# Attention in a macaron block: probabilities times V as three split passes for the 256-column blocks, with a new order of a head pair

## The chip, the cores and the metric

The kernel runs on one core of one Trainium2 chip. The metric is the device time of one execution in microseconds (us), lower is better; the time of a kernel is the median of its runs. TensorE (PE) multiplies 128x128 stationary weights with a moving operand and writes to the accumulation memory (PSUM, eight banks of 128x512 fp32). VectorE (DVE) and ScalarE (ACT) read and empty PSUM, GpSimd (POOL) works on the on-chip memory only, SyncE (SP) issues transfers. Each engine runs its own program in order, and they meet at semaphores.

## The reference, cut to what matters

```
x = x + 0.5 * ffn(layernorm(x))          # mixture of 8 experts (top 2) and a shared one
x = x + attention(layernorm(x))          # x: 4 batches x 256 tokens x 256
x = x + 0.5 * ffn(layernorm(x))

def attention(x):                        # 16 heads of 128
    q, k, v = x @ W_Q + b_Q, x @ W_K + b_K, x @ W_V + b_V
    scores = q @ k.T / sqrt(128)         # causal mask within 256 tokens
    z = softmax(scores) @ v
    return z @ W_O + b_O
```

All of it is in fp32. Where the kernel works with "split operands", a value is held as a high part that the faster fp32r format represents and a low part, the difference; a product is then three passes, high x high, high x low and low x high.

## The kernel before

The first feed-forward stage, the attention and the second feed-forward stage follow each other, each in its own block of instructions with a meeting of all engines between them. The change is in `attention()` alone.

The attention runs over 8 pairs of heads (pair 0 written out, the others in loops on each engine; on some engines the last pair is written out too). Within a pair the work is named by letter and number, and four strings give each engine the order of its own items: `ORDER` (PE), `ACT_ORDER`, `DVE_ORDER`, `POOL_ORDER` (lines 1224 to 1233). The numbers stand for these items:

- A0 to A3, B0 to B3: projections to Q and K of the two heads, for the first (A) and second (B) 512 tokens, 6 passes of 512 columns each. ACT or DVE adds the bias and writes `qk`.
- V0 to V3: projection to V for batch 0 to 3, both heads, 12 passes of 256 columns. ACT (V0, V2) or DVE (V1, V3) copies all 512 columns to `v`.
- S, K, E, R, P, T, M, Z, L, each with a unit number 0 to 7 (unit u is batch u // 2, head u % 2). S: scores on PE, fp32, a 128x128 block for the first 128 queries and a 128x256 block for the others. K: mask and row minimum on DVE (`masked`). E: exponential with row sum on ACT (`exps`). R: reciprocal on DVE (`recip`). P: product with it on POOL (`probs`). T: three 128x128 transposes on PE (`turn`), then a copy of the 384 columns to `pT` on ACT (`turned`). M: probabilities times V on PE (`mix`), fp32: keys 0 to 127 against all 256 queries, then keys 128 to 255 against the last 128. Z and L: high and low part of the result, on ACT (`z_high`) and DVE (`z_low`).
- O0 to O3: output projection of a batch, 12 passes of 256 columns, added to `x_res` on DVE (`added`). O3 of a pair is done in the next pair; in pair 0 its place on DVE holds the second half of the layer norm's application, and PE skips it.
- w0 to w5: POOL splits a sixth of the next pair's projection weights (`split_qkv`, two instructions of 256 columns). W0: the same for the output projection's weights (`split_out`), and in pair 0 also the addition of the output bias to `x_res` (`out_bias`, line 1291).

A, B, V and O write to banks 0 and 1 in turn (`BANKED`, `BANK`): item number n of that list waits until the item n - 2 has been emptied (`bank_free`, line 1477). In pair 0, where O3 is skipped, the item two places after it looks one further round back. Scores use banks 3 and 4, transposes 5 and 6, M banks 2 and 7. S0 waits for A0 to A3 to be written, S4 for B0 to B3 (`projected`). A pair begins on PE with a wait for the weights w0 to w3 (`s_ql`), V0 with one for w4 and w5. In pair 0 PE turns the second half of the normalised input before V0, ACT makes its high part (`norm_high`) and DVE its low part ahead of K0 (`norm_low`); B0 waits for both:

```python
if fresh and item == "K0":
    norm_low(dve, n, 1, (5, 6))
```

In the last pair DVE also takes the statistics of the next layer norm (ahead of L6, after O1 has been added) and applies it (ahead of O2); POOL computes the root in between.

## Time and profile before

| | us |
|---|---|
| median of 3 runs | 542.2 |
| the runs | 541.19, 542.2, 546.09 |
| the profiled execution | 542.72 |
| its span, first to last instruction | 540.8 |
| busy: PE / DVE / ACT / POOL | 515.3 / 326.7 / 268.6 / 273.6 |

The profile is one execution. Its times are in us from the span's start unless marked ns. A group of instructions is named by the line of the kernel, which may be that of a helper: L179 to L181 are the three passes of `split_matmuls`, L1560 and L1561 the two products of `mix`, L1542 the transposes, L1532 and L1533 the scores. An fp32 matmul leaves two records. The arrow gives the releaser of an idle time. A matmul is drawn until its modelled end, which lies past the start of the next.

### The profile page before, as it was taken

How to read it: one execution, taken by the hardware profiler on the slowest of the kernel's cores; microseconds unless marked ns; L12 is line 12 of the kernel's file. 1: busy time of each engine (PE TensorE's matmuls, PEld its weight loads, DVE VectorE, ACT ScalarE, POOL GpSimd, SP SyncE). 2: the span in 40 equal slices, each digit the busy share in tenths (PEclk: the TensorE clock that was granted, in tenths of full speed). 3: DMA queues.
4: the chain of work that ended last, by engine and by line, in shares of the span. 5: the costliest groups of instructions: out<-in, count | busy, mean ns of one | idle time of the engine just before them, and what ended most of it. 6: DMA issues, size and time to landing. Idle time of an engine off the chain costs nothing. (4 is left out here: it accounts for less than half of the span.)

```text
span 540.8 us, 10506 instructions
## 1 busy us (share of the span) xinstructions
PE 515.3 (95%) x3318; PEld 460.3 (85%) x3319; DVE 326.7 (60%) x821; ACT 268.6 (50%) x731; POOL 273.6 (51%) x364
## 2 busy tenths in 40 slices
PE   7999699997989999999999999999999799899996
PEld 4788599976879999898999998999999688799985
DVE  5689655548646564574655645746656768755537
ACT  3982356540554463563544635535456365355540
POOL 1737777751295372570843725718333221667750
PEclk9999799998999999999999999999999999999999
DMA  8941223342101001001010010010000140223327
GB/s 280 348 143 31 68 93 104 107 157 63 55 19 59 1 19 61 19 0 58 19 58 2 18 58 19 0 58 19 0 1 0 49 137 1 69 87 101 106 88 234
DMA packets 19401, 37.99 MB, mean 70 GB/s; under 512 B 2864, under 2 KB 10416, under 8 KB 19376
## 3 DMA queue, kind: packets, MB, share of 16 engines
q1 hardware_dynamic: 14960, 25.61, 14.4%
q0 software_dynamic: 4416, 12.06, 6.9%
q8 instruction: 14, 0.23, 0.2%
q14 instruction: 11, 0.09, 0.1%
HBM read 28.49 MB, written 9.18 MB: 70 GB/s over the span
## 5 line engine op out<-in xcount | busy, mean ns | idle before, releaser
L1315 POOL TENSOR_TENSOR s_a<-s_a,rr_a 128x128 f32<-128x128 f32 x64 | 25.5, 399 | 137.1 <-DVE rr_a L1422 137.1
L1362 ACT ACTIVATE s_a<-s_a,mn_a 128x128 f32<-128x128 f32 (+1 forms) x128 | 56.7, 446 | 14.9 <-DVE mn_a L1416 14.9
L179 PE MATMUL bank<-xT_h,area_h 128*128 128x512 f32 x128 | 53.7, 420 | 3.4 <-PEq L1171 3.4
L1412 DVE SCALAR_TENSOR_TENSOR s_a<-bank,cst 128x384 f32<-128x384 f32 x64 | 35.3, 551 | 35.3 <-PE bank L1533 35.1
L521 POOL DMA_INDIRECT xn<-x_normed,tok_i_f x46 | 45.7, 993 | 16.8 <-issue 10.2
L180 PE MATMUL bank<-xT_l,area_h 128*128 128x512 f32 x128 | 50.8, 397 | 0.0
L181 PE MATMUL bank<-xT_h,area_l 128*128 128x512 f32 x128 | 50.6, 396 | 0.0
L1355 ACT ACTIVATE qk_a<-bank,bias_a 128x512 f32<-128x512 f32 x32 | 21.9, 683 | 55.6 <-PE bank L181 55.6
L1367 ACT ACTIVATE pT_a<-bank 128x384 f32<-128x384 f32 x64 | 31.1, 486 | 34.5 <-PE bank L1542 33.6
L1404 DVE TENSOR_SCALAR qk_a<-bank,bias_a 128x512 f32<-128x512 f32 x32 | 24.0, 751 | 37.5 <-PE bank L181 37.5
L179 PE MATMUL bank<-area_h,xT_h 128*128 128x256 f32 x128 | 40.7, 318 | 0.0
L1428 DVE SCALAR_TENSOR_TENSOR area_l<-bank,bias_a,area_h 128x256 fp32r<-128x256 f32 x64 | 30.4, 477 | 17.0 <-ACT area_h L1372 17.0
L1416 DVE TENSOR_REDUCE mn_a<-s_a 128x1 f32<-128x128 f32 (+1 forms) x128 | 39.2, 347 | 2.2
L179 PE MATMUL bank<-w_h,xeT_h_f 128*128 x92 | 34.5, 375 | 5.6 <-DVE xeT_l_f L802 5.6
L1317 POOL TENSOR_TENSOR s_a<-s_a,rr_a 128x256 f32<-128x256 f32 x64 | 39.2, 612 | 0.0
L1560 PE MATMUL bank<-pT_a,v_a 128*128 128x256 f32 x128 | 39.1, 387 | 0.0
L179 PE MATMUL bank<-area_h 128*128 128x256 f32 x128 | 38.2, 298 | 0.6 <-issue 0.6
L527 POOL DMA_INDIRECT y_by_token<-rows_f,place_f x32 | 31.5, 985 | 13.4 <-issue 7.9
L1533 PE MATMUL bank<-qk_a 128*128 128x256 f32 x128 | 38.2, 381 | 0.0
L1372 ACT ACTIVATE area_h<-bank,bias_a 128x256 fp32r<-128x256 f32 x64 | 29.9, 467 | 14.2 <-PE bank L1561 14.2
L179 PE MATMUL bank<-xT_h,wgu_h 128*128 128x512 f32 x88 | 35.8, 407 | 1.0 <-DVE hT_l_f L706 1.0
L181 PE MATMUL bank<-area_h,area_l 128*128 128x256 f32 x128 | 36.3, 283 | 0.0
(176 smaller groups left out, 1652.3 us busy)
## 6 DMA issues: line engine op xcount, KB each, us to landing
area<-in_wqkv SPq DMA_DIRECT2D x8, 768.0 KB, 4.4
xn<-y_by_token SPq DMA_DIRECT2D x12, 256.0 KB, 3.7
w_r<-in_w SPq DMA_DIRECT2D x8, 352.0 KB
area_r<-in_w SPq DMA_DIRECT2D x16, 176.0 KB
x_normed<-xn SPq DMA_DIRECT2D x4, 512.0 KB, 5.8
area<-in_wo SPq DMA_DIRECT2D x8, 256.0 KB, 2.6
x_res<-in_x_in SPq DMA_DIRECT2D x4, 256.0 KB, 4.1
wgu_r<-in_wgu SPq DMA_DIRECT2D x4, 256.0 KB
```

Of the source, the lines that this page charges most:

```text
L179: pe.matmul(psum, lhs[0], rhs[0], start=first, stop=False)
L180: pe.matmul(psum, lhs[0], rhs[1], start=False, stop=False)
L181: return pe.matmul(psum, lhs[1], rhs[0], start=False, stop=last)
L521: pool.indirect_dma_start(xe[m % XR], None, xd, bass.IndirectOffsetOnAxis(ap=tok_i[:, m:m + 1], axis=0)).then_inc(s_xe[m % XR], 16)
L527: pool.indirect_dma_start(yd, bass.IndirectOffsetOnAxis(ap=place[:, m:m + 1], axis=0), ye[m % YR], None).then_inc(s_yst[m % YR], 16)
L1317: pool.tensor_tensor(s[b][:, P:3 * P], s[b][:, P:3 * P], rr[:, b, 1:2].to_broadcast([P, 2 * P]), ALU.mult).then_inc(s_p, 1)
L1362: act.activation(s[b][:, cols], s[b][:, cols], ACT.Exp, bias=mn[:, b, t:t + 1], scale=-1.0, accum_out=rs[:, b, t:t + 1]).then_inc(s_e, 1)
L1367: act.activation(pT[u % 2][:, :], bank[5 + u % 2][:, 0:3 * P], ACT.Copy).then_inc(s_ptv, 1)
L1412: dve.scalar_tensor_tensor(s[b][:, :], bank[3 + u % 2][:, 0:3 * P], -INV_SCALE, cst[:, C_MASK:C_MASK + 3 * P], ALU.mult, ALU.max).then_inc ...
L1416: dve.tensor_reduce(mn[:, b, t:t + 1], s[b][:, cols], op=ALU.min, axis=AX.X).then_inc(s_mn, 1)
L1533: pe.matmul(b[:, P:3 * P], q[:, t0 + P:t0 + 2 * P], k[:, t0:t0 + 2 * P], start=True, stop=True).then_inc(s_sc, 1)
L1560: pe.matmul(bank[ZB[u % 2]][:, 0:2 * P], v[:, 2 * bt, e], pT[u % 2][:, 0:2 * P], start=True, stop=False)
```

## The change

Three things are changed together. (1) The product with keys 0 to 127 (256 columns) is done in three fp32r passes from split operands; the product with keys 128 to 255 (128 columns) stays fp32. So V's even blocks are held as `v_h` and `v_l`, the odd ones as `v_odd`, and a transposed unit as `pT_h`, `pT_l` and `pT_odd`. (2) ACT copies the odd and the high part, two instructions for each V and each unit; DVE subtracts for the low part, after ACT, in V's items and in a new item Q (`turned_low`), with a new semaphore `s_ptl` that `turn` and `mix` wait on. V is now in ACT's and in DVE's list, and the counts `NA` and `ND` replace `PROJ // 2`. (3) The four orders are new; O3 stands second on PE and first on DVE; O1 on DVE stands behind Q6 and Q7; in the last pair the statistics are ahead of O2 and the application ahead of L7.

```diff
--- before.py
+++ after.py
@@ -1184,7 +1184,9 @@
                 qk = sb("qk", [P, 2, 2, TOK])
-                v = sb("v", [P, NT, 2 * DH])
+                v_h = sb("v_h", [P, BATCH, 2 * DH], FP32R)
+                v_l = sb("v_l", [P, BATCH, 2 * DH], FP32R)
+                v_odd = sb("v_odd", [P, BATCH, 2 * DH])
                 bias = sb("bias", [P, 3, 2])
@@ -1192,7 +1194,9 @@
                 rr = sb("rr", [P, NS, 2])
-                pT = [sb(f"pT{b}", [P, 3 * P]) for b in range(2)]
+                pT_h = [sb(f"pT_h{b}", [P, 2 * P], FP32R) for b in range(2)]
+                pT_l = [sb(f"pT_l{b}", [P, 2 * P], FP32R) for b in range(2)]
+                pT_odd = [sb(f"pT_odd{b}", [P, P]) for b in range(2)]
@@ -1210,6 +1214,7 @@
                 s_ptv = sem("a_pT")
+                s_ptl = sem("a_pT_low")
                 s_z = sem("a_z_psum")
@@ -1221,20 +1226,22 @@
-                ORDER = ("A0 A1 A3 A2 O3 V0 S0 S1 B0 S2 V1 T0 S3 V2 B3 T1 M0 B1 B2 T2 M1 S4 T3 M2 S5 S6 "
-                         "V3 M3 S7 T4 O0 T5 M4 M5 T6 O1 M6 T7 O2 M7").split()
-                ACT_ORDER = ("A0 A2 V0 E0 B0 E1 T0 V2 E2 E3 T1 Z0 B2 T2 Z1 T3 E4 Z2 E5 Z3 E6 T4 T5 E7 Z4 T6 "
-                             "Z5 T7 Z6 Z7").split()
-                DVE_ORDER = ("A1 A3 O3 K0 K1 R0 R1 V1 K2 K3 B3 R2 B1 L0 R3 K4 L1 K5 R4 K6 R5 K7 L2 R6 L3 V3 "
-                             "O0 R7 L4 L5 O1 L6 O2 L7").split()
-                POOL_ORDER = "w4 w5 P0 P1 W0 P2 w0 P3 w1 w2 w3 P4 P5 P6 P7".split()
+                ORDER = ("A0 O3 A1 A2 A3 V0 S0 S1 B0 S2 V1 B2 T0 S3 V2 T1 B1 B3 M0 T2 S4 S5 M1 T3 S6 V3 S7 M2 T4 "
+                         "M3 T5 O0 M4 M5 O1 T6 T7 O2 M6 M7").split()
+                ACT_ORDER = ("A0 A2 V0 B0 E0 E1 V1 T0 B2 E2 V2 T1 E3 Z0 T2 E4 T3 E5 Z1 V3 T4 Z2 Z3 T5 E6 E7 Z4 Z5 "
+                             "T6 T7 Z6 Z7").split()
+                DVE_ORDER = ("O3 A1 A3 V0 K0 K1 R0 K2 V1 R1 Q0 K3 V2 R2 Q1 B1 R3 B3 L0 K4 K5 R4 Q2 Q3 K6 R5 L1 K7 "
+                             "Q4 L2 Q5 L3 R6 V3 O0 R7 L4 L5 Q6 Q7 O1 O2 L6 L7").split()
+                POOL_ORDER = ("w4 w5 P0 P1 P2 P3 w0 W0 P4 P5 w1 P6 P7 w2 w3").split()
                 BANKED = [item for item in ORDER if item[0] in "ABVO"]
...
                 ON_DVE = [item for item in DVE_ORDER if item[0] in "ABV"]
+                NA, ND = len(ON_ACT), len(ON_DVE)
                 PROJECTED = [item for item in ORDER if item[0] in "ABV"]
@@ -1338,8 +1345,6 @@
                     kind, x = item[0], int(item[1])
-                    if kind == "V":
-                        return v[:, 2 * x:2 * x + 2, :].rearrange("p a b -> p (a b)")
                     half = "AB".index(kind)
@@ -1350,7 +1355,8 @@
                         if item[0] == "V":
-                            act.activation(proj_out(item), src, ACT.Copy).then_inc(s_pa, 1)
+                            act.activation(v_odd[:, x, :], src[:, 2 * DH:4 * DH], ACT.Copy)
+                            act.activation(v_h[:, x, :], src[:, 0:2 * DH], ACT.Copy).then_inc(s_pa, 1)
                         else:
@@ -1364,7 +1370,8 @@
                         act.wait_ge(s_pt, U * i + u + 1)
-                        act.activation(pT[u % 2][:, :], bank[5 + u % 2][:, 0:3 * P], ACT.Copy).then_inc(s_ptv, 1)
+                        act.activation(pT_odd[u % 2][:, :], bank[5 + u % 2][:, 2 * P:3 * P], ACT.Copy)
+                        act.activation(pT_h[u % 2][:, :], bank[5 + u % 2][:, 0:2 * P], ACT.Copy).then_inc(s_ptv, 1)
@@ -1399,7 +1406,9 @@
                         if item[0] == "V":
-                            dve.tensor_copy(proj_out(item), src).then_inc(s_pv, 1)
+                            dve.wait_ge(s_pa, NA * i + ON_ACT.index(item) + 1)
+                            dve.tensor_tensor(v_l[:, x, :], src[:, 0:2 * DH], v_h[:, x, :].bitcast(FP32),
+                                              ALU.subtract).then_inc(s_pv, 1)
                         else:
@@ -1421,6 +1430,11 @@
+                    def turned_low(i, u):
+                        dve.wait_ge(s_ptv, U * i + u + 1)
+                        dve.tensor_tensor(pT_l[u % 2][:, :], bank[5 + u % 2][:, 0:2 * P], pT_h[u % 2][:, :].bitcast(FP32),
+                                          ALU.subtract).then_inc(s_ptl, 1)
                     def z_low(i, u):
@@ -1442,11 +1456,11 @@
                                 dve.wait_ge(s_bo, 16 + BATCH)
-                            if last and item == "L6":
+                            if last and item == "O2":
...
                                 norm_stats(dve, norm3, 0)
-                            if last and item == "O2":
+                            if last and item == "L7":
                                 norm_apply(dve, norm3, 0)
@@ -1456,7 +1470,7 @@
                             else:
-                                {"K": masked, "R": recip, "L": z_low, "O": added}[kind](i, x)
+                                {"K": masked, "R": recip, "Q": turned_low, "L": z_low, "O": added}[kind](i, x)
@@ -1482,20 +1496,22 @@
                             at -= 2
+                            if at < 2:
+                                return
                         prior = BANKED[at - 2]
...
                             pe.wait_ge(s_ov, BATCH * pair + (int(prior[1]) + 1) % BATCH)
-                        elif prior in ON_ACT:
-                            pe.wait_ge(s_pa, (PROJ // 2) * pair + ON_ACT.index(prior) + 1)
+                        elif prior in ON_DVE:
+                            pe.wait_ge(s_pv, ND * pair + ON_DVE.index(prior) + 1)
                         else:
-                            pe.wait_ge(s_pv, (PROJ // 2) * pair + ON_DVE.index(prior) + 1)
+                            pe.wait_ge(s_pa, NA * pair + ON_ACT.index(prior) + 1)
...
-                        pe.wait_ge(s_pa, (PROJ // 2) * i + max(ON_ACT.index(x) + 1 for x in items if x in ON_ACT))
-                        pe.wait_ge(s_pv, (PROJ // 2) * i + max(ON_DVE.index(x) + 1 for x in items if x in ON_DVE))
+                        pe.wait_ge(s_pa, NA * i + max(ON_ACT.index(x) + 1 for x in items if x in ON_ACT))
+                        pe.wait_ge(s_pv, ND * i + max(ON_DVE.index(x) + 1 for x in items if x in ON_DVE))
@@ -1537,7 +1553,7 @@
                         if u >= 2:
-                            pe.wait_ge(s_ptv, U * i + u - 1)
+                            pe.wait_ge(s_ptl, U * i + u - 1)
                         for c in range(3):
@@ -1545,20 +1561,18 @@
                         bt, h = unit(u)
-                        pe.wait_ge(s_ptv, U * i + u + 1)
+                        pe.wait_ge(s_ptl, U * i + u + 1)
                         if h == 0:
-                            item = f"V{bt}"
-                            if item in ON_ACT:
-                                pe.wait_ge(s_pa, (PROJ // 2) * i + ON_ACT.index(item) + 1)
-                            else:
-                                pe.wait_ge(s_pv, (PROJ // 2) * i + ON_DVE.index(item) + 1)
+                            pe.wait_ge(s_pv, ND * i + ON_DVE.index(f"V{bt}") + 1)
                         if u >= 2:
...
                         e = slice(h * DH, (h + 1) * DH)
-                        pe.matmul(bank[ZB[u % 2]][:, 0:2 * P], v[:, 2 * bt, e], pT[u % 2][:, 0:2 * P], start=True, stop=False)
-                        pe.matmul(bank[ZB[u % 2]][:, P:2 * P], v[:, 2 * bt + 1, e], pT[u % 2][:, 2 * P:3 * P],
+                        z = bank[ZB[u % 2]]
+                        split_matmuls(pe, z[:, 0:2 * P], (v_h[:, bt, e], v_l[:, bt, e]),
+                                      (pT_h[u % 2][:, :], pT_l[u % 2][:, :]), True, False)
+                        pe.matmul(z[:, P:2 * P], v_odd[:, bt, e], pT_odd[u % 2][:, :],
                                   start=False, stop=True).then_inc(s_z, 1)
@@ -1569,8 +1583,9 @@
-                            assert BANKED[-2] == "O1" and BANK["O1"] == BANK["O3"]
-                            pe.wait_ge(s_ov, BATCH * i + 2)
+                            prior = [item for item in BANKED if BANK[item] == BANK["O3"]][-1]
+                            assert prior in ("O1", "O2")
+                            pe.wait_ge(s_ov, BATCH * i + int(prior[1]) + 1)
                         else:
```

## Rows read from the trace of the kernel before

**Rows 1.** busy time in three stretches: start:end, length, busy us (xinstructions) by engine, clock

```profile
132.27:172.13 39.86, 37.73 (x229) 32.95 (x229) 23.18 (x63) 19.87 (x56) 23.91 (x36) 0.96 0.11 31
243.80:279.63 35.83, 35.83 (x235) 32.72 (x233) 20.37 (x52) 17.89 (x54) 17.84 (x30) 1.00 0.08 29
422.96:429.09 6.13, 3.24 (x23) 2.33 (x21) 4.35 (x10) 1.56 (x3) 0.91 (x1) 1.00 0.00 0
```

**Rows 2.** timeline, PE, one pair: start us, drawn us, engine line op

```profile
252.02 0.28 PE L181 MATMUL bank<-area_h,xT_l 128*128 128x256 f32 x1
252.14 0.39 PE L1532 MATMUL bank<-qk_a 128*128 128x128 f32 x2
252.36 0.60 PE L1533 MATMUL bank<-qk_a 128*128 128x256 f32 x2
252.80 0.27 PE L1532 MATMUL bank<-qk_a 128*128 128x128 f32 x1
...
261.06 0.60 PE L1560 MATMUL bank<-pT_a,v_a 128*128 128x256 f32 x2
261.49 0.39 PE L1561 MATMUL bank<-pT_a,v_a 128*128 128x128 f32 x2
```

**Rows 3.** timeline, DVE and ACT, mask and exponentials of one unit

```profile
253.00 0.56 DVE L1412 SCALAR_TENSOR_TENSOR s_a<-bank,cst 128x384 f32<-128x384 f32 x1 [1.41 <-PE bank L1533]
...
254.24 0.40 ACT L1362 ACTIVATE s_a<-s_a,mn_a 128x128 f32<-128x128 f32 x1 [1.30 <-DVE mn_a L1416]
...
255.13 0.67 ACT L1355 ACTIVATE qk_a<-bank,bias_a 128x512 f32<-128x512 f32 x1
```

**Rows 4.** timeline, ACT and PE, the release of S4

```profile
264.67 0.69 ACT L1355 ACTIVATE qk_a<-bank,bias_a 128x512 f32<-128x512 f32 x1 [2.05 <-PE bank L181]
...
265.73 0.60 PE L1533 MATMUL bank<-qk_a 128*128 128x256 f32 x2
```

**Rows 5.** groups by line and form, whole span: count | busy us, mean ns | idle before

```profile
L1367 ACT ACTIVATE pT_a<-bank 128x384 f32<-128x384 f32 x64 | 31.1, 486 | 34.5 <-PE bank L1542 33.6
L583 ACT ACTIVATE xeT_h_f<-bank 128x256 fp32r<-128x256 f32 x46 | 17.5, 380 | 0.1
L802 DVE TENSOR_TENSOR xeT_l_f<-bank,xeT_h_f 128x256 fp32r<-128x256 f32 x46 | 19.5, 423 | 23.4 <-ACT xeT_h_f L583 23.4
L1404 DVE TENSOR_SCALAR qk_a<-bank,bias_a 128x512 f32<-128x512 f32 x32 | 24.0, 751 | 37.5 <-PE bank L181 37.5
...
L1278 POOL TENSOR_TENSOR area_h<-area,cst 128x256 fp32r<-128x256 f32 x42 | 25.8, 614 | 3.3 <-PE bank L181 3.3
L1281 POOL TENSOR_TENSOR area_l<-area,area_h 128x256 fp32r<-128x256 f32 x42 | 31.1, 739 | 3.3
```

**Rows 6.** timeline, PE and ACT, start of pair 0

```profile
132.27 0.75 PE L179 MATMUL bank<-xT_h,area_h 128*128 128x512 f32 x1 [3.40 <-PEq L1171]
...
134.52 0.63 PE L181 MATMUL bank<-xT_h,area_l 128*128 128x512 f32 x1
134.95 0.63 PE L179 MATMUL bank<-xT_h,area_h 128*128 128x512 f32 x1
...
135.25 0.69 ACT L1355 ACTIVATE qk_a<-bank,bias_a 128x512 f32<-128x512 f32 x1 [5.36 <-PE bank L181]
...
142.95 1.28 ACT L1362 ACT_TABLE_LOAD   x1
```

**Rows 7.** timeline, POOL and PE, output projection's weights and bias in pair 0

```profile
147.89 1.04 POOL L1303 TENSOR_TENSOR area_h<-area,cst 128x512 fp32r<-128x512 f32 x1
...
150.26 5.00 POOL L1295 TENSOR_TENSOR x_res<-x_res,bo_sb_a 128x512 f32<-128x512 f32 x4
...
156.25 0.55 PE L1542 MATMUL bank<-cst,s_a 128*128 128x128 f32 x3 [1.69 <-POOL s_a L1317]
```

**Rows 8.** timeline, DVE, end of pair 7

```profile
420.09 0.69 DVE L1435 TENSOR_TENSOR x_res<-x_res,bank 128x512 f32<-128x512 f32 x1
...
423.90 1.38 DVE L219 TENSOR_SCALAR xn<-x_res,mv,rstd 128x256 f32<-128x256 f32 x4 [1.04 <-POOL rstd L214]
```

## The prediction

> **What bounds the kernel now.** I read the page first: TensorE (PE) busy for 95% of the span, no other engine above 60%. Then the busy time in stretches, cut at the first matmul of A0 of a head pair [rows 1]: a middle pair takes 35.83 us (pairs 1 to 6: 35.83 to 35.87) and PE is busy in all of it, VectorE (DVE) 20.4, ScalarE (ACT) 17.9, GpSimd (POOL) 17.8. In these pairs every matmul saved is time saved, as long as the other engines give their results in time. Pair 0 takes 39.86 and has gaps, and 6.13 us pass from the last M7 to the next stage: there the order of waits is the bound. Then the timeline. A matmul is drawn longer than its distance to the next, so I go by starts [rows 2]: one fp32r pass of 256 columns, its own weight load with it, takes 0.12; the fp32 product of 128 columns (two records) 0.22, of 256 columns 0.43 to 0.44; a unit's three transposes 0.33. From starts like these A or B (6 passes of 512) is 1.37, V or O (12 passes of 256) 1.43, a unit's scores 0.66, its mix 0.65.
>
> **How a result travels.** The first scores really end at 252.80 [rows 2] and DVE masks them from 253.00 [rows 3]: 0.20 from PE to a consumer. ACT ends B2 at 265.36 and the second part of the scores S4 starts at 265.73, 0.06 later than without a wait [rows 4]: the first part took its 0.22 from 265.51 on, so PE goes on 0.15 after its releaser. DVE and ACT start some 0.04 after a releaser; back to back their instructions overlap by 0.1. From the mask's start to the exponentials 1.24 pass, and these occupy ACT for 0.89 [rows 3]; the product with the reciprocals takes POOL 0.96.
>
> **Edit 1, three passes for the 256 columns.** 3 x 0.12 = 0.36 in place of 0.435: -0.075 a unit, **-0.60 a pair**, -4.8 in all. No row has a pass with pT moving; the nearest (256 columns, 128x128 weights, both fp32r) has its size. Bounds: half of a 512-column pass (0.114, -6 in all), and half of the fp32 product, 0.22, if the format saves nothing (+14). I take the nearest. The Trainium skill ("FP8 and Floating Point Precision", TensorE Precision Notes) says that true FP32 is four passes; by that rule three would cost three quarters of 0.435, 0.33, and the edit -7. The row's pass is dearer than a quarter, so the row decides.
>
> **Edit 2, more evacuation.** ACT copies each transposed unit in two pieces (128 and 256 columns) instead of one of 384 that took 0.486; 256 columns take 0.380 [rows 5], so 128 columns 0.27, and with the overlap a unit occupies ACT for 0.47 instead of 0.39. Bounds 0.39 (second piece free) and 0.66 (no overlap). All four V go through ACT, 0.57 each. DVE has 12 subtractions of 0.42 a pair [rows 5] more and two copies less: busy 24 of 35; ACT 21. Neither becomes the bound. What counts is what is queued behind a late piece: behind V0's low half K0 and K1, behind Q0 K3, behind Q2 and Q3 K6.
>
> **The order of a pair, walked.** Counted from A0's start without a wait: A0 ends at 1.37, O3 2.80, A3 6.91, V0 8.34, S1 9.66, B0 11.03, S2 11.69, V1 13.12, B2 14.49, T0 14.82, V2 16.91, B1 18.61, B3 19.98, M0 20.56, T2 20.89, S5 22.21, V3 25.21, M2 26.45, T4 26.78, T5 27.69, O0 29.12, M5 30.28, O1 31.71, T7 32.37, O2 33.80, M7 34.96. Against it:
> - T0, due at 14.49: V0's low half keeps DVE until 9.6, K0 ends 10.8; ACT does B0 before E0, so E0 ends 12.8, P0 14.0. Slack 0.35.
> - S4, due at 20.89, needs B3 from DVE: 19.98 + 0.20 + 0.75 [rows 5] + 0.15 = 21.08. **A new wait of 0.19**, since M0 (0.36 + 0.22) and T2 (0.33) cover only 0.91 of the 1.10; S5, M1 and T3 stand behind it. It was 0.06. Later marks move by 0.19.
> - ACT does T4, Z2, Z3, T5, E6, E7 in a run: 27.17 + 0.47 + 0.38 + 0.38 + 0.47 + 0.88 + 0.88 = 30.63. L3 ends at 29.82, M5 waits 0.08, about as now. P5, P7, L1 and V3's low half come 0.04 to 0.15 before T5, T7, M3 and O1 want them.
> - O3 is now second: L7 of the pair before ends 1.19 after A0's start, +0.15 = 1.34 against 1.37.
> - A0 needs w3, which POOL now splits after P7: E7 30.7, R7 31.1, P7 32.1, w2 and w3 2 x 1.39: 34.8 + 0.15 against M7's end at 35.2. Slack 0.26.
> A middle pair: -0.60 + 0.13 = -0.47, 35.36 us. Six of them: **-2.8**.
>
> **Pair 0.** The same order meets waits that the loop doesn't have.
> (a) O3 is skipped but keeps its place in the alternation of the two banks, so A1 gets A0's bank and waits for ACT, which ends at 135.25 + 0.69 = 135.94 [rows 6]. A1 starts at 136.09 instead of 134.95: +1.14. In return A1 is wholly past the slow clock (1.37, it took 1.74) and the 8 transposes find their input ready (0.87, they took 1.2). V0 ends at 142.50 instead of 142.07.
> (b) The two subtractions for xT's low half stand before K0 on DVE, and V0's low half is now ahead of them. It ends at 143.8, they (0.69 each) at 145.03; B0 starts at 145.18, due at 143.81: 1.37.
> (c) ACT does B0 before E0, so the exp table's load of 1.28 [rows 6], now in a hole, comes after B0: 147.44 + 1.28, E0 ends 149.7, P0 150.9, T0 at 151.05, due at 150.0: 1.05.
> (d) POOL adds the output bias behind W0, 5.0 us in a run [rows 7]. In the kernel before P2 is behind it, and T2 waits 1.69 [rows 7]. After the change P4 is: P3 ends at 157.2, w0 takes 1.39 (0.61 and 0.74 and their gaps [rows 5]), W0 2.37, the bias 5.0 [rows 7], P4 0.96: 166.9. T4 starts at 167.07 and is due at 163.20. **A gap of 3.9 us.**
> From T4's start 8.5 to M7's end: pair 1 starts at 175.6 against 172.13, **+3.5**. Bounds: +1.5 if (c) is hidden and W0 or w0 partly ahead, +5 if the recovery after T4 has waits too.
>
> **The end.** The next stage's statistics follow O1's addition, which on DVE now stands behind Q6 and Q7. Before, it ended 33.66 after the pair's A0 (420.78 less 387.12, the same cut as in the other pairs), and the normalisation came 3.12 later [rows 8]. Now Q7 ends at 34.0, O1 at 34.62, the normalisation starts at 37.74 instead of 36.78. Only L7 is left behind it (O2 and L6 lie under POOL's root), which gives 0.6 back: O3 and its addition end 0.4 later, counted from the pair's start, M7's gain included. **+0.4** for pair 7 and the end.
>
> **The sum.** +3.5 - 2.8 + 0.4 = +1.1. The profiled execution took 542.72 (span 540.8, 1.9 around it), 0.5 above the median of 542.2; from it 543.8, from the median 543.3. I say 543.5.
>
> **Rivals.**
> *The clock falls in the gap of (d).* After 3.4 us without a matmul PE came back at 1.2 GHz, half its clock (0.96 granted over pair 0, 1.00 in a middle pair [rows 1]), and 512-column passes took 0.43 instead of 0.23 [rows 6]; seven of them cost 1.5 us. 3.9 us may do the same: 545.0. The wait of (a) may also hold back the rise, at the same price. The Trainium skill ("TensorE: Matmul & The Clock Gate", HAM oscillation) says that an idle TensorE goes back to half clock; by it the fall is sure and the sum +2.6. One gap in this trace agrees. 0.22.
> *Late links, on the slower side.* If ACT's two pieces don't overlap (0.66 instead of 0.47), the run from T4 to E7 grows by 0.4 or more and uses up the slacks of M5, T5, T7 and A0. A pair loses some 0.7 at these, 7 pairs 4.9: 548.5. It decides the sign from 0.6 a pair. For it: slacks of 0.04 to 0.15 in a walk that is good to 0.05 a step. Against: ACT's neighbours overlap everywhere in the timeline. 0.17.
> *Pair 0 is milder,* +1 instead of +3.5: 541. For it: transfers and splits that I may place wrongly; against: bias and bank order stand in program order. 0.13.
> *The passes stay at 0.22:* the change doesn't do what it says, +14, 556. Against: V's and O's passes beside fp32 neighbours run at 0.12. 0.02.
> My forecast holds 0.46, with a range of its own of 541.5 to 545.5.
>
> **Range and chances.** From a mild pair 0 with no new wait in the pairs (542.2 + 1 - 4 = 539.2) to half of the late links with the fallen clock (547.5): 539.5 to 548. About 1% (5.4 us) is what a measurement of this kernel can tell from no change; the three runs lie 4.9 apart. Faster by over 1% needs all of edit 1 and nothing given back: 0.03. Slower by over 1%: the late links, the passes, or the clock's fall with small waits: 0.2. Within: 0.77.
>
> **What would show it.** Right: middle pairs of 35.36; S4 with 0.19 of wait; A1 at 136.1, B0 at 145.2; T4's transposes after 3.9 us idle, released by POOL's product; pair 1 at 175.6; 42.4 us from the last A0 to the next stage (42.0 now). Wrong: a middle pair above 35.8, a pair 0 under 41 us, or passes of another size than 0.12.

## The result, and the profile after

| | median, us | runs | lowest to highest |
|---|---|---|---|
| before | 541.84 | 6 | 541.19 to 546.09 |
| after | 548.96 | 6 | 547.49 to 554.01 |

The ratio is 1.0135, with an interval of 1.0075 to 1.0195: slower, by 7.1 us. It is clear of no change, but whether it is over 1% the interval leaves open. The forecast of 543.5 and its range of 539.5 to 548 are missed. The profiled execution took 547.49, with a span of 545.7.

Busy time in stretches of the kernel after, cut at the first matmul of A0 as in [rows 1] (start:end, length, busy us and instructions of PE, PEld, DVE, ACT, POOL, then the granted clock, DMA share, GB/s): pair 0, a middle pair, the end behind the last M7 (with its last few matmuls), and three stretches taken out of them.

```profile
132.51:177.20 44.69, 38.09 (x236) 34.12 (x237) 26.04 (x72) 21.51 (x70) 22.36 (x34) 0.92 0.10 27
248.04:283.46 35.42, 35.42 (x244) 32.55 (x242) 23.51 (x62) 19.23 (x69) 17.97 (x31) 1.00 0.10 30
...
132.51:136.00 3.49, 2.63 (x10) 1.88 (x11) 2.05 (x11) 0.69 (x1) 1.22 (x2) 1.00 0.56 98
...
164.90:171.70 6.80, 5.46 (x26) 5.47 (x27) 2.36 (x7) 3.68 (x14) 4.49 (x9) 0.50 0.00 0
...
427.70:431.10 3.40, 2.99 (x14) 2.96 (x15) 2.28 (x6) 1.08 (x2) 0.00 (x0) 0.51 0.00 0
```

The middle pair is the forecast one within 0.06. Pair 0 is 4.9 longer, the forecast was 3.5. (Before, A0 of pair 1 starts at 172.05 and pair 0 is 39.78; the cut of 172.13 in [rows 1] lies 0.08 behind that.) And two stretches of this kernel's attention run at half clock (0.50 is 1.2 GHz): one around T4's start in pair 0, and one around the last transposes at the end. Before, both places had 1.00, and only pair 0's beginning was slow, which here, in this execution, is not.

Timeline of the kernel after, PE, at the waits that were forecast for pair 0 (start, drawn length, engine, line, operation, idle before and its releaser): A1, B0, T0, and T4 with what follows it.

```profile
135.00 0.50 PE L179 MATMUL bank<-xT_h,area_h 128*128 128x512 f32 x1 [0.86 <-ACT qk_a L1361]
...
144.38 0.47 PE L179 MATMUL bank<-xT_h,area_h 128*128 128x512 f32 x1 [1.34 <-issue]
...
150.32 0.55 PE L1558 MATMUL bank<-cst,s_a 128*128 128x128 f32 x3 [0.87 <-POOL s_a L1324]
...
166.24 0.90 PE L1558 MATMUL bank<-cst,s_a 128*128 128x128 f32 x3 [3.53 <-POOL s_a L1324]
166.79 0.56 PE L179 MATMUL bank<-pT_h_a,v_h_a 128*128 128x256 f32 x1
167.15 0.41 PE L180 MATMUL bank<-pT_l_a,v_h_a 128*128 128x256 f32 x1
167.36 0.41 PE L181 MATMUL bank<-pT_h_a,v_l_a 128*128 128x256 f32 x1
167.57 0.63 PE L1575 MATMUL bank<-pT_odd_a,v_odd_a 128*128 128x128 f32 x2
```

All four waits are there, in the order and about of the size that was forecast; an idle time is measured from a drawn end, so each is some 0.2 shorter than the real standstill. From T4 on the passes start 0.21 apart instead of 0.12: the clock is down. POOL, in the same stretch, is what T4 waited for: W0, the bias in one run, then P4 and P5.

```profile
157.92 1.04 POOL L1310 TENSOR_TENSOR area_h<-area,cst 128x512 fp32r<-128x512 f32 x1
159.04 1.28 POOL L1313 TENSOR_TENSOR area_l<-area,area_h 128x512 fp32r<-128x512 f32 x1
160.28 4.97 POOL L1302 TENSOR_TENSOR x_res<-x_res,bo_sb_a 128x512 f32<-128x512 f32 x4
165.22 0.39 POOL L1322 TENSOR_TENSOR s_a<-s_a,rr_a 128x128 f32<-128x128 f32 x1
165.57 0.61 POOL L1324 TENSOR_TENSOR s_a<-s_a,rr_a 128x256 f32<-128x256 f32 x1
```

The end, timeline of the kernel after, first DVE, where [rows 8] had the addition at 420.09 and the application at 423.90, then PE:

```profile
423.83 0.68 DVE L1449 TENSOR_TENSOR x_res<-x_res,bank 128x512 f32<-128x512 f32 x1
424.54 1.41 DVE L195 BATCH_NORM_STATS2 stats<-x_res 128x6 f32<-128x256 f32 x4
...
427.64 1.38 DVE L219 TENSOR_SCALAR xn<-x_res,mv,rstd 128x256 f32<-128x256 f32 x4 [0.45 <-POOL rstd L214]
```

```profile
424.96 0.38 PE L1575 MATMUL bank<-pT_odd_a,v_odd_a 128*128 128x128 f32 x2
428.11 1.97 PE L227 MATMUL bank<-cst,xn 128*128 128x128 f32 x8 [2.77 <-DVE xn L219]
```

PE stands still for 2.77 ahead of the next stage's transposes (the same wait was 1.25 before), and the eight transposes that follow are drawn over 1.97, at half clock.

The granted clock of all runs says the same. With a mean clock m, a run of T us has spent 2 x (1 - m) x T at half clock: the median of the six runs has 0.9795, 22.5 us; the kernel before, on the chip of the first experiments, 0.988, 13.0 us. What such a microsecond costs can be read off two runs of the kernel after: 547.49 at 0.983 (18.6 us) and 554.01 at 0.970 (33.2 us), 6.5 in 14.6 or 0.45 us each. Of the 7.1 us, 9.5 x 0.45 = 4.3 would then be clock. That is a correlation; the experiments test it.

### The profile page after: what moved, and what is told of

It is laid out like the page before. It is cut to its first block and busy times, and to the rows that moved or that the text cites. A ratio compares the mean times of both kernels' runs of the same rounds, so it can differ in the third digit from the quotient of the medians.

```text
span 545.7 us, 10845 instructions
## 1 busy us (share of the span) xinstructions
PE 513.4 (94%) x3382; PEld 462.0 (85%) x3383; DVE 351.6 (64%) x901; ACT 280.0 (51%) x843; POOL 274.7 (50%) x364
## 5 line engine op out<-in xcount | busy, mean ns | idle before, releaser
L1435 DVE TENSOR_TENSOR pT_l_a<-bank,pT_h_a 128x256 fp32r<-128x256 f32 x64 | 26.5, 421 | 23.6 <-ACT pT_h_a L1374 23.4
L179 PE MATMUL bank<-area_h 128*128 128x256 f32 x128 | 39.8, 311 | 0.0
L180 PE MATMUL bank<-area_l,area_h 128*128 128x256 f32 x128 | 36.9, 289 | 0.0
L181 PE MATMUL bank<-area_h,xT_l 128*128 128x256 f32 x128 | 36.2, 283 | 0.0
L180 PE MATMUL bank<-area_l,xT_h 128*128 128x256 f32 x128 | 36.1, 282 | 0.0
```

Source lines behind the costliest of these rows:

```text
L179: pe.matmul(psum, lhs[0], rhs[0], start=first, stop=False)
L180: pe.matmul(psum, lhs[0], rhs[1], start=False, stop=False)
L181: return pe.matmul(psum, lhs[1], rhs[0], start=False, stop=last)
L1435: dve.tensor_tensor(pT_l[u % 2][:, :], bank[5 + u % 2][:, 0:2 * P], pT_h[u % 2][:, :].bitcast(FP32), ALU.subtract).then_inc(s_ptl, 1)
```

## The experiments

Twelve kernels, in four sets, each set with runs of the kernel before beside it. The sets did not all run on the same chip: in the first and the last the kernel before took 543.4 and 544.2, in the second and the third 572.8 and 572.0, with the difference in the feed-forward stages. So kernels are compared by their ratios to the kernel before, and by the lengths of the attention's pairs. This table has them all, each length from the one profiled execution, with the mean granted clock of that stretch in brackets (from the busy time in stretches of each kernel); "last" is the last pair with the end, up to the next stage. The stage behind the attention, which no edit touches, took 111.0 to 113.8 us in the seven profiled executions where the kernel before took 542 to 544, so effects of 1 or 2 us are read from the pairs and not from a whole profiled time.

| kernel | pair 0 (clock) | middle pair | last (clock) | ratio, interval |
|---|---|---|---|---|
| before | 39.78 (0.96) | 35.83 | 42.04 (1.00) | 1 |
| after | 44.69 (0.92) | 35.41 | 43.40 (0.96) | 1.0135, 1.0075 to 1.0195 |
| e1_bias | 39.74 (0.96) | 35.41 | 43.33 (0.96) | 1.0011, 0.9979 to 1.0043 |
| e2_warm | 46.23 (0.90) | 35.42 | 42.60 (1.00) | 1.0044, 1.0011 to 1.0077 |
| e3_fp32mix | 49.36 (0.83) | 35.89 | 43.75 (0.96) | 1.0164, 1.0097 to 1.0231 |
| e4_before_bias | 38.44 (0.92) | 35.83 | 43.28 (0.96) | 0.9967, 0.9928 to 1.0007 |
| e5_pair0 | 37.59 (0.92) | 35.41 | 43.77 (0.96) | 0.9934, 0.9909 to 0.9959 |
| e6_all | 36.47 (0.95) | 35.60 | 42.06 (1.00) | 0.9945, 0.9916 to 0.9975 |
| e8_tail | 46.16 (0.89) | 35.41 | 42.98 (0.96) | 1.009, 1.0057 to 1.0124 |
| e9_best | 36.24 (0.96) | 35.47 | 41.94 (1.00) | 0.9898, 0.985 to 0.9946 |
| e10_order | 37.22 (0.93) | 35.27 | 41.72 (1.00) | 0.9877, 0.982 to 0.9933 |
| e11_fill | 34.66 (1.00) | 35.27 | 41.75 (1.00) | 0.982, 0.9767 to 0.9873 |
| e12_before_fill | 35.62 (1.00) | 35.83 | 42.05 (1.00) | 0.9908, 0.9877 to 0.9939 |
| e13_after_fill | 38.54 (1.00) | 35.41 | 42.60 (1.00) | 0.9927, 0.9892 to 0.9961 |

### The bias away from the products with the reciprocals

The changed kernel with one thing moved; the same edit is made to the kernel before as e4.

```diff
@@ pool: pair 0
+                    out_bias()
                     body(0, "first")
@@ pool: behind W0
-                        if more == "first":
-                            out_bias()
```

> The changed kernel with one step moved: POOL adds the output bias at the start of pair 0, ahead of P0, while it idles, and not between W0 and P4. My theory (the gap before T4 in pair 0 costs 3.5 us itself and lets TensorE's clock fall, which costs 2.75 more): T4 waits for nothing, no half clock in pair 0, pair 0 about 6 us shorter (38.5 us), all in all 6.3 us less: 542.7. Rival 1 (the clock falls whether or not there is this gap): 3.5 us less, 545.5. Rival 2 (the loss is in the pairs of the loop): no more than 1 us less, 548. Middle pairs stay at 35.41 in all.

> The kernel before with the output bias moved to the start of pair 0. My theory (its waits before T2 and T3 in pair 0, 1.69 and 0.44 us, are this addition's): 2.1 us less, 539.7. Rival (T2 and T3 are then held by W0, which stays ahead of P2): 0.5 to 1 us less.

Measured: e1 543.85 at a ratio of 1.0011, 1.2% less than the kernel after, and e4 541.3 at 0.9967. Timeline of e1, POOL, where the bias now stands, and PE at T4, which now follows M2 without a gap:

```profile
136.64 5.04 POOL L1302 TENSOR_TENSOR x_res<-x_res,bo_sb_a 128x512 f32<-128x512 f32 x4 [1.64 <-DVE xn L219]
```

```profile
162.97 0.38 PE L1574 MATMUL bank<-pT_odd_a,v_odd_a 128*128 128x128 f32 x2
163.19 0.49 PE L1557 MATMUL bank<-cst,s_a 128*128 128x128 f32 x3
163.44 0.36 PE L179 MATMUL bank<-pT_h_a,v_h_a 128*128 128x256 f32 x1
163.64 0.28 PE L180 MATMUL bank<-pT_l_a,v_h_a 128*128 128x256 f32 x1
163.76 0.28 PE L181 MATMUL bank<-pT_h_a,v_l_a 128*128 128x256 f32 x1
```

Behind T4 the second and third pass start 0.12 apart, where the kernel after has 0.21: the clock did not fall there. The middle pairs stay at 35.41, so both rivals are out. Some 6.7 us of the loss (1.24% of 543) hang on where four additions stand on an engine that is busy half the time. To the kernel before the same move gives 0.3%, with an interval that reaches to no gain at all. In e4's trace no wait is left ahead of T2 and T3, as its theory had it, and pair 0 is 1.34 shorter although some 6 us at its start were at half clock instead of 3.4.

### The standstill kept, its clock paid for

The changed kernel with products that nobody reads, put where PE would stand still: 30 of 256 columns ahead of T4 in pair 0, 24 ahead of the last transposes. Nothing is left out; the waits themselves stay.

```diff
+                            elif fresh and item == "T4":
+                                turn(i, x, 30)    # keep_warm, then the wait
@@ behind the last pair
+                    keep_warm(pe, 3, 24)
                     norm_turn(pe, norm3, 0, (3, 4))
```

> The changed kernel with filling products on TensorE, whose results nothing uses: 30 of 256 columns (0.11 us each) ahead of T4's wait in pair 0, and 24 ahead of the last stage's transposes after pair 7. No wait is shorter. My theory (two of the changed kernel's losses are stretches at half clock behind gaps of 3.5 and 2.8 us): the clock stays up at both places, 2.75 + 1.0 = 3.8 us less, 545.2; T4 starts where it did. Rival (the falls have another cause): time as the changed kernel, 549, with half clock at the same places.

Measured: 546.19, a ratio of 1.0044, 0.9% less than the kernel after (1.0011 to 1.0077 against 1.0075 to 1.0195: the intervals just touch). Timeline of e2, PE, around T4:

```profile
167.50 0.38 PE L1578 MATMUL bank<-pT_odd_a,v_odd_a 128*128 128x128 f32 x2
167.72 3.44 PE L187 MATMUL bank<-rank_w 128*128 128x256 bf16 x30
171.47 0.55 PE L1561 MATMUL bank<-cst,s_a 128*128 128x128 f32 x3 [0.31 <-POOL s_a L1324]
171.77 0.36 PE L179 MATMUL bank<-pT_h_a,v_h_a 128*128 128x256 f32 x1
171.97 0.28 PE L180 MATMUL bank<-pT_l_a,v_h_a 128*128 128x256 f32 x1
172.09 0.28 PE L181 MATMUL bank<-pT_h_a,v_l_a 128*128 128x256 f32 x1
```

T4 is as late behind M2 as in the kernel after, but at full clock, and pair 1 starts 8.53 behind it (180.00 less 171.47), the 8.5 of the forecast. In the kernel after it is 10.96 (177.20 less 166.24). **2.43 us is what the fall of the clock in that gap cost**, by this pair of traces; the forecast's rival had 1.5. The last pair with the end is 42.60 instead of 43.40: 0.80 for the second fall. Pair 0 of this execution is nevertheless long, because its beginning was slow:

```profile
133.77:143.20 9.43, 8.59 (x19) 6.25 (x20) 3.85 (x14) 0.86 (x2) 1.22 (x2) 0.50 0.30 97
```

9.4 us at half clock at the start of the pair, against 3.4 in e1 and in the kernel before and none in the kernel after, although PE had stood still for 3.4 there too. From A0's start to the second transposes of the norm this makes 10.64, 7.94 and 6.75 us with the same instructions. The start differs from execution to execution and costs up to 3.9. The rival, that the falls have another cause, is out: both places where the products stand have 1.00.

### The passes undone alone

The changed kernel with `mix` in fp32, everything else kept, the extra copies and subtractions too (the low parts are then zero and not used).

```diff
... v_h and pT_h are declared fp32 and not fp32r
-                        split_matmuls(pe, z[:, 0:2 * P], (v_h[:, bt, e], v_l[:, bt, e]),
-                                      (pT_h[u % 2][:, :], pT_l[u % 2][:, :]), True, False)
+                        pe.matmul(z[:, 0:2 * P], v_h[:, bt, e], pT_h[u % 2][:, :], start=True, stop=False)
```

> The changed kernel with the three passes undone alone: V's even blocks and the transposed units are copied as fp32 by the same instructions in the same order, the subtractions stay (they give zeros that nothing uses), and the 256 columns are one fp32 product again. My theory (the passes save 0.075 us a unit, and the loop's pairs are bound by TensorE): middle pairs 35.41 + 0.60 = 36.0, 4.8 us more, 553.8. Rival (the pairs are held by the evacuations and not by TensorE): middle pairs stay near 35.4 and the time at 549.

Measured: 553.93, a ratio of 1.0164. The middle pair is 35.89 against 35.41: the passes are worth 0.48 a pair net. Timeline, PE, M4 in the kernel after and in e3:

```profile
277.62 0.28 PE L179 MATMUL bank<-pT_h_a,v_h_a 128*128 128x256 f32 x1
277.74 0.28 PE L180 MATMUL bank<-pT_l_a,v_h_a 128*128 128x256 f32 x1
277.86 0.28 PE L181 MATMUL bank<-pT_h_a,v_l_a 128*128 128x256 f32 x1
277.98 0.38 PE L1575 MATMUL bank<-pT_odd_a,v_odd_a 128*128 128x128 f32 x2
```

```profile
284.99 0.60 PE L1573 MATMUL bank<-pT_h_a,v_h_a 128*128 128x256 f32 x2
285.42 0.38 PE L1574 MATMUL bank<-pT_odd_a,v_odd_a 128*128 128x128 f32 x2
```

Three passes take 0.36 from start to start and the fp32 product 0.43 to 0.44, which is some 0.60 a pair; in exchange the waits at S4 and M5 shrink, from 0.21 to 0.13 and from 0.08 to nothing. So the passes do what the forecast said, and the loss of the kernel after is none of theirs. The intervals of e3 and of after overlap, so the whole times don't show this, the pairs do.

### The other waits of pair 0

e5: on top of e1, A1 of pair 0 takes bank 7 and not A0's, DVE makes xT's low half ahead of V0's, ACT does E0 ahead of B0, the three waits (a), (b), (c) of the forecast.

```diff
-                    body(0, ACT_ORDER[2:])
+                    body(0, " ".join(ACT_ORDER[2:]).replace("B0 E0", "E0 B0").split())
-                            if fresh and item == "K0":
+                            if fresh and item == "V0":
-                        b = bank[BANK[item]]
+                        b = bank[7 if fresh and item == "A1" else BANK[item]]
... DVE reads A1 from bank 7 too, and A3 waits for A0's bank in place of A1
```

> The bias moved as in e1_bias and the other three waits of pair 0 taken away by changing what makes them: A1 of pair 0 alone writes to the idle bank 7, xT's low half is subtracted ahead of V0's low half, and ACT does E0 (with the table load before it) ahead of B0. My theory (1.1, 1.4 and 1.05 us of wait, less what the faster start gave back; and these gaps keep TensorE at half clock at the start of pair 0, up to 10.2 us instead of 3.4 in two of the executions seen): pair 0 is 37.1 us with 3.4 us at half clock, 2.6 us less than e1_bias, and the mean granted clock of its runs rises from 0.984 towards 0.988: 540.5. Rival (they lie one behind the other and only the longest counts): 1.4 us less than e1_bias and the same clock: 542.4.

Measured: 568.99 against 572.81, 0.9934. Pair 0 is 37.59 with a mean clock of 0.92, and PE is drawn busy in all 37.59 of it, where e1 has 36.69 busy of 39.74. So all three waits are gone, and pair 0 is 2.15 shorter than in e1 although its slow stretch at the start was longer (some 6 us, where theory had 3.4); the rival's 1.4 is too small. This version of the changed kernel is faster than the kernel before.

### Three changes of order

e8 alone has DVE's "O1" ahead of "Q6 Q7" in the changed kernel; e6 has e5, this, and M1 ahead of S4; e9 has e6 and O3 behind A1 (and A2 of pair 0 without a wait for its bank); e10 has e9 and the evacuation of M1 (Z1 and L1) earlier.

```diff
-"... Q4 L2 Q5 L3 R6 V3 O0 R7 L4 L5 Q6 Q7 O1 O2 L6 L7"   # DVE: e8, and e6, e9, e10
+"... Q4 L2 Q5 L3 R6 V3 O0 R7 L4 L5 O1 Q6 Q7 O2 L6 L7"
-"A0 O3 A1 ... M0 T2 S4 S5 M1 T3"                         # PE: M1 e6, O3 e9
+"A0 A1 O3 ... M0 T2 M1 S4 S5 T3"
-"... Z0 T2 E4 T3 E5 Z1 V3 ..."                           # ACT: e10 (DVE: L1 behind R4, R5 ahead of K6)
+"... Z0 T2 Z1 E4 T3 E5 V3 ..."
```

> The changed kernel with O1's addition ahead of Q6 and Q7 on DVE, in all pairs, and nothing else. My theory: the statistics start 0.7 us sooner, the next stage starts 42.7 us after the last A0 (43.4 now), 548.2; middle pairs as before at 35.41. Rival (Q7, now later, holds M7 and the next A0): middle pairs above 35.5 and no gain, 549 or more.

> As e5_pair0, and M1 ahead of S4 (0.58 us more between B3 and S4), and O1's addition on DVE ahead of Q6 and Q7. My theory (S4 waits 0.21 in each pair for B3; the end's normalisation follows O1's addition): middle pairs 35.41 - 0.21 = 35.20 us, the last pair and the end 0.7 less: 2.2 us less than e5_pair0, 538.3. Rival (what is taken away at S4 returns at the next wait, M5 or T5, whose slacks are under 0.1): middle pairs 35.35 to 35.41, 540.

> As e6_all, and O3 behind A1 instead of ahead of it on PE and DVE (A1 and A2 of pair 0 without a bank to wait for). My theory (O3 waits 0.14 us in each pair for L7 of the pair before, which A0 alone doesn't cover): middle pairs 35.20 - 0.14 = 35.06, 1 us less than e6_all: 537.3, a ratio to the kernel before of 0.99. Rival (w3 on POOL is as late as L7, and A0 waits instead): as e6_all.

> The kernel of e9_best with the evacuation of M1 one place earlier on ScalarE and two places earlier on VectorE. In e9 M3 waits about 0.46 us in each pair for the areas that M1 and the row products before it leave, and nothing else in the pair waits that long. Theory: the wait is only an order, and it goes: the seven later pairs take 35.05 to 35.15 us each against 35.47, pair 0 stays at 36.1 to 36.4, the whole gains 2 to 3 us on e9 and stands 1.2 to 1.6 per cent under the kernel before. Rival: ScalarE or VectorE is what bounds that stretch, the wait moves to Q2, Q3 or T3, and the pairs stay at 35.4 to 35.5: then no more than 0.5 us over e9.

Measured: e8 1.009. Against after's 1.0135 the intervals overlap, so alone it isn't shown by the whole time; the last pair with the end is 42.98 against 43.40, and PE's idle time ahead of the last transposes 2.04 against 2.77. In e6 the end was 42.06 with a clock of 1.00, 1.7 less than in e5, and pair 0 1.1 less, where the slow stretch at the start was 3.4 us instead of 6.8, but each middle pair was 0.19 longer. In the profiled executions e6's attention is 1.7 shorter in all and the stage behind it 2.4 longer, and the ratios (0.9945 and 0.9934) can't be told apart. Moving M1 took S4's wait of 0.21 away and made another, timeline of e6:

```profile
281.78 0.46 DVE L1444 SCALAR_TENSOR_TENSOR area_l<-bank,bias_a,area_h 128x256 fp32r<-128x256 f32 x1
...
282.36 0.19 PEld L179 LDWEIGHTS bank<-pT_h_a,v_h_a 128*128 128x128 f32 x1 [0.43 <-issue]
282.39 0.36 PE L179 MATMUL bank<-pT_h_a,v_h_a 128*128 128x256 f32 x1 [0.23 <-DVE area_l L1444]
```

M3 waits until M1's bank is empty, and L1 stands late in DVE's order. e9 took O3's wait (35.47, where 35.06 was expected, without M3's new wait), e10 M3's (35.27; the expectation had 35.05 to 35.15, and two waits of 0.11 and 0.15, at M4 and M5, are what is left). In the time e10 is at 0.9877 and e9 at 0.9898, which the intervals don't tell apart.

### The clock held at both ends of the attention

20 unused products behind the norm ahead of pair 0 and 18 ahead of the last transposes: e11 is e10 with them, e13 is e1 with them (the changed kernel, its orders untouched), e12 is e4 with them (the kernel before), the control.

```diff
                         norm_turn(pe, after, 0, (4, 5))
+                        keep_warm(pe, 1, 20)
@@ behind the last pair
+                    keep_warm(pe, 3, 18)
```

> The kernel of e10_order with unused products on TensorE in the two stretches in which it would stand still: 20 of 256 columns behind the norm ahead of the attention, and 18 behind the last pair ahead of the next stage. Nothing of the computation is left out. Theory: the clock falls after such standing still, and half of what the changed kernel lost was that: pair 0 begins at the full clock (its first passes 0.12 to 0.23 us and not 0.44), no stretch near the end of the attention is at half clock, and the time is 1.5 to 3 us under e10. Rival: the clock falls by something else than gaps (the load of the core over a longer time), so that it falls elsewhere instead, the mean granted clock is that of e10 within 0.003, and the time is that of e10 or up to 1 us more.

> The kernel before with the output bias made at the start of pair 0 and the same two sets of unused products: the control of e11. Theory: what the fillers give they give both kernels; the kernel before gains 2 to 4 us by the two together (1.4 at the start, up to 1 at the end, 1.3 by the bias). Its middle pairs stay at 35.83, so that e11 stays some 4 to 6 us under it, 0.4 of each pair by the passes and 0.35 by the orders. Rival: the fillers only repair what the change broke, and the kernel before is within 1 us of its time without them.

> The changed kernel with the output bias made at the start of pair 0 and the two sets of unused products of e11, no order changed: e1_bias with fillers, and the counterpart of e12_before_fill (ratio 0.9908 to the kernel before). Theory: with the clock held at the start and the end and the standing still ahead of T4 gone, only the three small waits of pair 0 (1.1, 1.4 and 1.0 us) and the new waits of each pair are left of the loss, and they about cancel the 0.42 us that each of six later pairs gains: pair 0 takes 38.2 to 38.5 us against 35.62 in e12, the later pairs 35.41 against 35.83, the last with the end 0.3 to 0.6 more than e12's 42.05, in all +0.2 to +0.8 us on e12, a ratio of 0.990 to 0.994. Rival: the waits of pair 0 let the clock fall there although the fillers stand ahead of it, pair 0 takes 39.7 us or more, and the ratio is 0.996 to 1.001, that of e1_bias.

Measured: e11 562.13 (0.982), e12 567.73 (0.9908), e13 539.44 (0.9927). Pair 0 and the last pair with the end, busy time in stretches, e13 and then e12:

```profile
131.65:170.19 38.54, 35.44 (x236) 31.68 (x237) 25.86 (x72) 21.06 (x70) 21.92 (x33) 1.00 0.12 32
382.69:425.29 42.60, 40.69 (x282) 36.61 (x280) 29.13 (x80) 20.97 (x72) 13.70 (x24) 1.00 0.00 0
```

```profile
147.65:183.27 35.62, 35.62 (x228) 31.96 (x229) 23.08 (x63) 19.79 (x56) 24.11 (x36) 1.00 0.11 34
398.27:440.32 42.05, 40.59 (x274) 36.87 (x272) 25.91 (x69) 19.45 (x57) 11.30 (x20) 1.00 0.00 0
```

With the clock at 1.00 in every pair of both kernels, the change can be read without it, and without the bias's gap: 38.54 - 35.62 = +2.9 in pair 0 (three waits of 3.56 by the forecast, less 0.6 for the passes: 2.96), 6 x -0.42 = -2.5 in the middle, +0.55 at the last, **+0.95 in all**, just above the 0.2 to 0.8 expected. The forecast's +1.1 isn't the sum to hold against this: it had the bias's gap in it and the waits that the bias made before. Its terms for these two kernels are 2.96 - 2.8 + 0.4 = +0.6. The ratios of e13 and e12 can't be told apart, as theory had it. Against e1, which has the same orders and no fillers, e13 is 0.8% less (0.9927 and 1.0011, intervals apart): of the 4.4 between the profiled executions pair 0 gives 1.2 and the last pair 0.7, where the products stand, and 2.2 lie in the stage behind, whose scatter is as large; the median of the mean clock is 0.992 instead of 0.9835. The kernel before gains 4.3 us by the bias and the products (e12), so the products don't only repair what the change broke, which was e12's rival.

e11 is the best version: 1.8% under the kernel before, and 1.0% under e12 (562.13 against 567.73 in one set, 5.6 us, the intervals just apart: by the profiles 0.96 in pair 0, 6 x 0.56 = 3.4 in the middle, 0.3 at the last; the rest isn't placed). In this set e11 is 2.9 under e10 (the intervals of the ratios overlap), and pair 0 gives 2.56 of it by the profiles. The mean clock rose too, from 0.9755 to 0.979 in the medians, just beyond the rival's 0.003, and both ends of the attention have 1.00: nothing shows that it fell elsewhere instead.

## Why the prediction was wrong

**The middle pair: right, with two small errors that partly cancel.** 35.41 against 35.36 forecast. A fp32r pass with pT moving is 0.12, as taken from the nearest row; the other bounds (0.114, 0.22) are out. S4 waits 0.21 (0.19 forecast). M5 waits 0.08 as forecast, but that isn't "about as now": read the same way, it was 0.19 before. And O3, for which the walk had 1.34 against 1.37, has a wait of 0.14. So -0.60 + 0.15 - 0.11 + 0.14 = -0.42, where -0.47 was forecast. A slack of 0.03 was called cover in a walk that is good to 0.05. The walk itself ended at 34.96 + 0.19 + 0.08 = 35.2, 0.13 under the 35.36 that was forecast from the kernel before; O3's wait is about that. ACT's pieces took 278 and 388 ns (0.27 and 0.38 forecast) and overlap; the late links are out.

**Pair 0: the waits right.** A1 at 2.49 behind A0's start (1.37 of work, 1.12 of wait; 1.14 forecast), B0 after a standstill of 1.5 (1.37), T0 after 1.0 (1.05), each counted from the real end of the work ahead of it. With the bias out of the way T4 starts 30.04 after A0 (e13), with it 33.73: 3.69, where 3.9 was forecast. Pair 1 is 8.50 behind T4 in e13. So the 44.69 of the kernel after are 30.04 + 3.69 + 8.50 + 2.46, and the last term is the clock.

**The step that failed: the clock, kept out of the sum as a rival of 0.22, with one place and 1.5 us.** The runs showed two places, 2.46 us and 0.80 us. The clock fell in gap (d) in all three kernels whose profile has that gap unfilled (after 3.53, e3 3.38, e8 3.55), and there in none without it. The forecast had the evidence in its own rows: 3.4 us without a matmul and half the clock behind it [rows 1, 6]; a gap of 3.9 was forecast next to it, and the fall should have been part of the likeliest case. Its price came from seven passes at the start of pair 0, when the slow stretch there was 3.43 long; the one at (d) was 6.8, of which PE worked 5.46, and the passes in it started 0.21 apart instead of 0.12. And it had a second place, which the forecast didn't name: the change delays the application at the end by O1's place and gains on M7, so PE stands still for 2.77 instead of 1.25 ahead of the last transposes, and the clock fell there too, 0.80.

The Trainium skill ("TensorE: Matmul & The Clock Gate", HAM oscillation) was quoted in the forecast with "by it the fall is sure", and for gap (d) the three traces that have it agree. The gap ahead of pair 0 in the kernel after doesn't: 3.40 of idle time, 1.00 behind it. So "sure" was too strong, and 0.22, for a fall that came in three of three, too low. Beside it, Part 1 of the same page says of the warm-up that it is "run-variable", by the phase at the kernel's start. Here, behind a gap in the middle of the kernel, the time at half clock varied as well: 0, 3.4 and 9.4 us at pair 0's start with the same instructions.

**The sum with those terms.** 543.8 (the sum against the profiled execution) + 2.46 for (d) + 0.80 at the end + 7 x 0.05 in the pairs (35.41 against 35.36) - 1.2 for a start that in this execution was at full clock + 1.1 for what lies outside the attention (the start 0.24, the rest 0.9, which is within the scatter of that stage) = 547.3; measured 547.49. That is still inside the range of 539.5 to 548. The median is 1.5 above that execution, and its mean clock is 0.9795 against 0.983: 3.9 us more at half clock, at 0.45 each 1.8. The two profiled executions lie 4.8 apart, and the 7.1 of the medians holds this 1.5 and another 0.9, by which the profiled execution of the kernel before lies above its median.

**The end.** +0.4 forecast. O1's addition ended 34.82 after the pair's A0 (34.62) and the application started after 37.95 (37.74); without the fall it is 42.60 against e12's 42.05 and the 42.04 of before: +0.56.

**The chances.** 0.2 for slower by over 1% was held by the late links first, which are out, and by the passes. The fallen clock was reckoned at 545.0, inside "within 1%"; with both falls at their measured price, 3.3 instead of 1.5, that case would have stood at 547 and at the edge of "slower".

**What stays open.** Why a slow stretch at pair 0's start lasted 3.4 us in one execution and longer in another. Counted from the fall, which can lie in the idle time ahead, it was 3.4 in the kernel before, e1, e6, e8 and e9, 6.8 in e4, e5 and e10, 10.2 in e2 and e3, and none in the kernel after. Whether the wait of A1 holds back the rise was not settled: e4, e5 and e10, which don't have it, had 6.8; both executions with 10.2 do have it, and so do e1 and e8 with 3.4 and the kernel after with none. How much of the run-to-run scatter of one kernel is this start isn't shown either: profiles are single executions.

## What to carry to other kernels

When a change opens a gap in TensorE's work, look for a gap of that length in the trace of before and see what the clock did behind it: if it fell, the fall belongs in the likeliest case, at every place where the change makes PE stand still, and its price comes from the work that follows the gap. Before an order is moved, look at what else stands in the same engine's program in the one pass of the loop that is written out: a bias addition of 5 us that cost about 0.3%, if anything, in one order cost 1.2% in another. And a slack smaller than the error of the walk is a wait.

## What the runs showed of the hardware

- Whether the clock falls in a gap is not decided by its length alone. Ahead of pair 0, with an idle time of 3.0 to 3.4, it fell in ten of eleven executions, and not in that of the kernel after. Ahead of the last transposes an idle time of 2.6 to 2.8 had the fall behind it in after, e1, e3 and e5, one of 2.04 in e8 but not in e6, e9 and e10, and one of 1.25 in e4 but not in the kernel before. With unused products in the gap (e2, e11, e12, e13) it never fell.
- Unused products held the clock: 30 of 256 columns in 3.44 us kept it at 1.00, and cost the waiting work next to nothing (T4 starts 3.75 behind the end of M2 with them, 3.69 without).
- The stretches at half clock in the attention were 3.4, 6.8 or 10.2 us long: 6.8 at gap (d) in all three kernels, 3.4 ahead of the next stage in all six kernels where it fell. A price read from a stretch of 3.4 was too low for one of 6.8.
- A microsecond at half clock cost 0.45 of a microsecond over the kernel after's runs, and 2.43 in 6.8 (0.36) at gap (d) and 0.80 in 3.4 (0.24) at the end of the kernel after, where PE still waited in part of the stretch.
